# A fused two-layer sequence block on one core: values, next projections, transposes and gates at other half-steps, rounded rows taken from the bank, all second stacks issued by SyncE

## What is computed

```python
def _ada_rmsnorm(x, t, gamma_w, beta_w):
    return (t @ gamma_w.T)[:, None, :] * _rmsnorm(x) + (t @ beta_w.T)[:, None, :]
...
xa = _ada_rmsnorm(x, t, attn_gamma_w, attn_beta_w)
q, k, v = split(xa @ W_q.T), split(xa @ W_k.T), split(xa @ W_v.T)      # 16 heads of 16
attn = softmax(scale * einsum('bnqd,bnkd->bnqk', q, k)); o = einsum('bnqk,bnkd->bnqd', attn, v)
x = x + a_alpha * (o @ W_o.T)
xf = _ada_rmsnorm(x, t, ffn_gamma_w, ffn_beta_w)
x = x + f_alpha * (silu(xf @ gate_w.T) * (xf @ hidden_w.T) @ out_w.T + out_b)
```

## Time and profile before

| | |
|---|---|
| median of 3 runs | 1057.74 us (1053.43 to 1057.96) |
| the profiled execution | 1055.76 us, its span 1054.0 us |
| TensorE busy, granted clock | 996.8 us (95%), 0.968 |
| VectorE, ScalarE, GpSimd busy | 761.7, 536.2, 269.4 us |

### The profile page before, as it was taken

One profiled execution on the slowest core, in us unless ns is written; L12 is line 12 of the kernel. 1 busy time (PEld: TensorE's weight loads), 2 busy tenths in 40 slices (PEclk: granted clock), 3 DMA queues, 4 the chain that ended last, 5 costly groups with the idle time before them and its releaser, 6 DMA issues.

```text
span 1054.0 us, 17114 instructions
## 1 busy us (share of the span) xinstructions
PE 996.8 (95%) x5402; PEld 618.3 (59%) x5402; DVE 761.7 (72%) x1214; ACT 536.2 (51%) x1119; POOL 269.4 (26%) x258
## 2 busy tenths in 40 slices
PE   6999999996999899989989998999899899989988
PEld 4777777773534455645655564556456555645677
DVE  5888788996577777678677767776875877587233
ACT  5466455453555555456445545554564555356421
POOL 1365422221000312132122213221321232122142
PEclk9999999997999899989999998999899899999999
DMA  9544574432420240313022212403130222120000
GB/s 288 144 104 128 141 155 116 120 95 71 111 62 7 59 113 2 81 50 66 11 70 68 47 34 63 98 1 80 51 66 11 72 65 32 62 51 7 11 16 21
DMA packets 93718, 75.11 MB, mean 71 GB/s; under 512 B 44881, under 2 KB 79769, under 8 KB 93665
## 3 DMA queue, kind: packets, MB, share of 16 engines
q1 hardware_dynamic: 79072, 57.20, 20.9%
q10 hardware_dynamic: 14592, 17.25, 7.2%
HBM read 27.73 MB, written 12.61 MB: 38 GB/s over the span
## 4 chain that ended last, share of the span: by engine, by line
PE 78%; DVE 12%; issue 4%; DMA 2%; SPq 1%; ACT 1%; POOL 0%; DVEq 0%; ACTq 0%; POOLq 0%
PE bank L1113 19%; PE bank L362 12%; PE bank L927 10%; PE bank L946 10%; PE bank L1157 8%; PE raw_pair L886 6%; PE bank L812 4%; DVE rowmax L894 3%; PE bank L1007 2%; DVE amax L444 2%; PE bank L385 1%; PE bank L1075 1%; PE bank L862 1%; DVE h L414 1%; DVE x_in L1059 1%
## 5 line engine op out<-in xcount | busy, mean ns | idle before, releaser
L894 DVE TENSOR_REDUCE rowmax<-raw_pair 128x2 f32<-128x1024 f32 x256 | 312.9, 1222 | 127.7 <-PE raw_pair L886 127.7
L935 ACT ACTIVATE probs<-bank 128x512 f32<-128x512 f32 x512 | 281.8, 596 | 230.0 <-PE bank L927 227.7
L886 PE MATMUL raw_pair<-k_stack,q_stack 48*128 48x512 f32 x512 | 177.3, 472 | 24.5 <-DVE rowmax L894 23.7
L927 PE MATMUL bank<-q_stack,k_stack 50*128 50x512 f32 x512 | 197.3, 456 | 2.4 <-DMA q_stack<-shift_rows 1.3
L362 PE MATMUL bank<-up_w,xs_part 128*128 128x512 f32 x768 | 193.3, 405 | 5.7 <-issue 4.5
L362 PEld LDWEIGHTS bank<-up_w,xs_part 128*128 128x128 f32 x768 | 143.4, 192 | 40.5 <-issue 7.4
L946 PE MATMUL bank<-probs,v_ext 128*17 128x512 f32 x1024 | 139.5, 618 | 1.4 <-ACT probs L935 1.2
L1143 POOL TENSOR_TENSOR hid<-scratch,hid 128x512 fp32r<-128x512 f32 x64 | 82.4, 1287 | 217.2 <-ACT hid L1139 217.2
L927 PEld LDWEIGHTS bank<-q_stack,k_stack 50*128 50x128 f32 x512 | 81.7, 190 | 87.4 <-issue 50.3
L1113 PE MATMUL bank<-xf_part,gate_w 128*128 128x512 f32 x384 | 106.0, 411 | 0.8 <-POOL xf_part L1098 0.8
L1113 PE MATMUL bank<-xf_part,hidden_w 128*128 128x512 f32 x384 | 105.3, 409 | 0.0
(11 more groups left out here) (138 smaller groups left out, 1135.1 us busy)
## 6 DMA issues: line engine op xcount, KB each, us to landing
q_stack<-split SPq DMA_DIRECT2D x48, 128.0 KB, 3.0
q_stack<-hid SPq DMA_DIRECT2D x48, 128.0 KB, 2.9
xk<-xT SPq DMA_DIRECT2D x32, 128.0 KB, 3.0
xt<-x_tok SPq DMA_DIRECT2D x32, 128.0 KB, 2.7
x_spill<-x1t ACTq DMA_DIRECT2D x32, 128.0 KB, 2.5
xa_spill<-xa ACTq DMA_DIRECT2D x32, 128.0 KB, 2.3
x_in<-xa_spill SPq DMA_DIRECT2D x8, 512.0 KB, 4.8
k_stack<-split ACTq DMA_DIRECT2D x32, 128.0 KB, 4.8
```

Of the source, the lines that this page charges most:

```text
L886: mm = nc.tensor.matmul(raw_pair[:, half, :], q_stack[rows, slot, qt * P:(qt + 1) * P], k_stack[rows, slot, :], start=True, stop=True)
L894: nc.vector.reduce_max(rowmax[:, e:e + RAWS + 1:RAWS], raw_pair[:], AX.X).then_inc(raw_read, 1)
L927: nc.tensor.matmul(score_bank[c % 3][:], k_stack[rows, slot, kt * P:(kt + 1) * P], q_stack[rows, slot, :], start=True, stop=True).then_inc ...
L935: nc.scalar.activation(probs[:, (kt % 2) * J + j, :], score_bank[c % 3][:], ACT.Exp).then_inc(exp_done, 1)
```

## The change

The table is filled anew: both value modules at half-step 1, q and k of the next batch at 4 and 5, the transposes at 6, the gates and hidden products from 8, and the eight pieces of the last product singly from 24. ScalarE instead of VectorE takes the values out of the banks (`v_act`), and splits the next input at half-step 2; the products of `normed_dve` are shared (two on VectorE, two on ScalarE in `normed_act`) and stand on VectorE ahead of half-step 5's maximum instead of behind it. The feed-forward scale and bias are copied to a tile (`affine_dve`). `xf_act` makes the rounded rows from the bank; `x_in`, which only the difference reads, comes behind it, half on VectorE, half on ScalarE. The first gate waits for the rounded rows, and for the two differences only ahead of the products that use them. SyncE issues all twelve DMAs of the second stacks. `sums_dve` has one more wait, for an operation of the half-steps before.

```diff
-        def split_xa_act(act, c, v_use=None):
+
+        def split_xa_act(act, c):
 
             act.wait_ge(xa_loaded, (c + 1) * 16)
-            if v_use is not None:
-                for m in range(2):
-                    act.wait_ge(pair_free[m], credited(pair_free[m], v_use[m] + 1))
...
-        def stack_sp(sp, m, uses, scores=None):
-
-            for w, rows in ((0, range(ROWS // HD)), (1, range(ROWS // HD - 2))):
+        def stack_sp(sp, m, uses, scores=None, all_rows=False):
+
+            for w in range(2):
                 sp.wait_ge(pair_free[w], credited(pair_free[w], uses[w] + 1))
                 if scores is not None:
                     sp.wait_ge(score_full, scores)
-                for r in rows:
+                for r in range(ROWS // HD - (2 if w == 1 and not all_rows else 0)):
...
-        def v_dve(dve, c, m, use):
-            dve.wait_ge(pv_done, credited(pv_done, c * 16))
-            dve.wait_ge(pair_full[m], use + 1)
-            nc.vector.tensor_scalar(v_ext[:, m * HALF:(m + 1) * HALF, :, 0:HD],
-                                    ab[m][:].rearrange("p (t h d) -> p t h d", t=HALF, d=HD), 1.0, None, ALU.mult) \
+        def v_act(act, c, m, use):
+            act.wait_ge(pv_done, credited(pv_done, c * 16))
+            act.wait_ge(pair_full[m], use + 1)
+            nc.scalar.activation(v_ext[:, m * HALF:(m + 1) * HALF, :, 0:HD],
+                                 ab[m][:].rearrange("p (t h d) -> p t h d", t=HALF, d=HD), ACT.Copy) \
...
         def normed_dve(dve, c, rows=None, normed=None):
             dve.wait_ge(rstd3_done, c + 1)
-            for t in range(T):
+            for t in range(HALF):
                 last = nc.vector.tensor_scalar((normed or normed_rows)(t), (rows or x2)[:, t, :], rstd3[:, t:t + 1], None, ALU.mult)
             last.then_inc(xn3_done, 1)
 
+        def normed_act(act, c, rows=None, normed=None):
+            act.wait_ge(rstd3_done, c + 1)
+            for t in range(HALF, T):
+                last = nc.scalar.activation((normed or normed_rows)(t), (rows or x2)[:, t, :], ACT.Copy,
+                                            scale=rstd3[:, t:t + 1])
+            last.then_inc(xn3_done, 1)
...
         def xf_pe(pe, c, use, normed=None):
-            pe.wait_ge(xn3_done, c + 1)
-            for k in reversed(range(KD)):
+            pe.wait_ge(xn3_done, 2 * c + 2)
+            for k in range(KD):
...
+        def affine_dve(dve, c):
+            nc.vector.tensor_copy(affine[:], par[:, c, FGAM:FGAM + 2 * KD]).then_inc(affine_ready, 1)
+
         def xf_dve(dve, c, use, splits):
 
             dve.wait_ge(q_in_low, credited(q_in_low, splits))
+            dve.wait_ge(affine_ready, c + 1)
+            dve.wait_ge(f_in_high, KD * c + 1)
+            nc.vector.tensor_scalar(x_in[:, :, 0, :], ab[0][:].rearrange("p (t n) -> p t n", t=T),
+                                    affine[:, 0:1], affine[:, KD:KD + 1], ALU.mult, ALU.add).then_inc(pair_free[0], 1)
+
+        def xf_act(act, c, use, splits):
+            act.wait_ge(affine_ready, c + 1)
             for k in range(KD):
-                dve.wait_ge(pair_full[k], use[k] + 1)
-            for k in reversed(range(KD)):
-                nc.vector.tensor_scalar(x_in[:, :, k, :], ab[k][:].rearrange("p (t n) -> p t n", t=T),
-                                        par[:, c, FGAM + k:FGAM + k + 1], par[:, c, FBET + k:FBET + k + 1],
-                                        ALU.mult, ALU.add).then_inc(pair_free[k], 1)
-
-        def xf_act(act, c, use):
-            for k in reversed(range(KD)):
-                act.wait_ge(pair_free[k], credited(pair_free[k], use[k] + 1))
-                nc.scalar.activation(xf_part[0][:, k, :].rearrange("p (t n) -> p t n", t=T), x_in[:, :, k, :],
-                                     ACT.Copy).then_inc(f_in_high, 1)
-
-        def xf_pool(pool, c):
-            for n, k in enumerate(reversed(range(KD))):
-                pool.wait_ge(f_in_high, KD * c + (n + 1))
+                act.wait_ge(pair_full[k], use[k] + 1)
+                nc.scalar.activation(xf_part[0][:, k, :], ab[k][:], ACT.Identity,
+                                     bias=affine[:, KD + k:KD + k + 1], scale=affine[:, k:k + 1]) \
+                    .then_inc(f_in_high, 1)
+            act.wait_ge(q_in_low, credited(q_in_low, splits))
+            nc.scalar.activation(x_in[:, :, 1, :], ab[1][:].rearrange("p (t n) -> p t n", t=T), ACT.Identity,
+                                 bias=affine[:, KD + 1:KD + 2], scale=affine[:, 1:2]).then_inc(pair_free[1], 1)
+
+        def xf_pool(pool, c, use):
+            for k in range(KD):
+                pool.wait_ge(pair_free[k], credited(pair_free[k], use[k] + 1))
...
         def hidden_pe(pe, c, n, f, use, spare=False):
-            pe.wait_ge(f_in_low, credited(f_in_low, KD * (c + 1)))
+            pe.wait_ge(f_in_high, KD * (c + 1))
             pe.wait_ge(pair_free[n], credited(pair_free[n], use + (max(f - 1, 0) if spare else f)))
             weight = (gate_w, hidden_w)[n]
-            for i, (a, wp, k) in enumerate(PROJECTION):
+            for i, (a, wp, k) in enumerate([(a, wp, k) for a, wp in PARTS for k in range(KD)]):
+                if n == 0 and f == 0 and a == 1:
+                    pe.wait_ge(f_in_low, credited(f_in_low, KD * c + (k + 1)))
...
-        V_AT, WO_AT, XF_AT, FFN_AT, OUT_AT = (1, 4), 2, 7, 10, 26
-        Q_AT, K_AT, TO_STACK = 8, 9, 16
-        SPLIT_XA_AT = V_AT[1] + 1
-        OUT_PIECES = ([(0, 0)], [(2, 0)], [(0, 1)], [(1, 0), (1, 1)], [(2, 1)], [(3, 0), (3, 1)])
-
-
-        LAST_PIECES = 4
+        WO_AT, XF_AT, FFN_AT, OUT_AT = 2, 6, 8, 24
+        QK0_AT, TO_STACK = (4, 5), 16
+        OUT_PIECES = ([(0, 0)], [(2, 0)], [(0, 1)], [(1, 0)], [(1, 1)], [(2, 1)], [(3, 0)], [(3, 1)])
+
+
+        LAST_PIECES = 5
...
                 if ffn and h == WO_AT + 3:
+                    affine_dve(dve, b - 1)
                     mean_dve(dve, b - 1)
+                    normed_dve(dve, b - 1)
...
-            stack_sp(sp, 1, both(u, at["qk1"]))
+            stack_sp(sp, 1, both(u, at["qk1"]), all_rows=True)
```

More of the change, by code:

```diff
@@ L1190, in plan @@
             table[0] = [("qk", 1, 0), ("qk", 1, 1)]
-            for m in range(2):
-                table[V_AT[m]] = [("v", m)]
+            table[1] = [("v", 0), ("v", 1)]
             if following:
-                table[Q_AT] = [("qk", 0, 0)]
-                table[K_AT] = [("qk", 0, 1)]
+                for w in range(2):
+                    table[QK0_AT[w]] = [("qk", 0, w)]
             if ffn:
@@ L1302, in act_batch @@
                         squares_act(act, b - 1, m)
-                if following and h == SPLIT_XA_AT:
-                    split_xa_act(act, b + 1, both(u, at["v"]))
-                if ffn and h == XF_AT + 1:
-                    xf_act(act, b - 1, both(u, at["xf"]))
+                if ffn and h == WO_AT + 2:
+                    normed_act(act, b - 1)
+                if ffn and h == XF_AT:
+                    xf_act(act, b - 1, both(u, at["xf"]), b + 2 if following else b + 1)
                 if following and h in (TO_STACK, TO_STACK + 1):
@@ L1338, in dve_batch @@
                     x2_dve(dve, b - 1, 0, u + at["wo"][0])
-                if ffn and h == WO_AT + 3:
-                    normed_dve(dve, b - 1)
+                if ffn and h == XF_AT:
+                    xf_dve(dve, b - 1, both(u, at["xf"]), b + 2 if following else b + 1)
                 for p in done:
@@ L1367, in pool_batch @@
                     normalise_pool(pool, b, 0)
+                if following and h == 2:
+                    split_xa_pool(pool, b + 1)
                 if ffn and h == WO_AT + 3:
                     rstd_pool(pool, b - 1)
-                if following and h == SPLIT_XA_AT:
-                    split_xa_pool(pool, b + 1)
-                if ffn and h == XF_AT + 1:
-                    xf_pool(pool, b - 1)
+                if ffn and h == XF_AT:
+                    xf_pool(pool, b - 1, both(u, at["xf"]))
                     bias_pool(pool, b - 1)
@@ L1456, in act_after @@
                 squares_act(act, B - 1, m, x1_in)
-            xf_act(act, B - 1, (END + 1, END + 1))
+            normed_act(act, B - 1, x1_in, last_normed_rows)
+            xf_act(act, B - 1, (END + 1, END + 1), B)
             for f in range(NH):
```

37 lines of the change are left out of this document (19 added, 18 removed).

## The result

The changed kernel takes **1036.99 us** (median of 4 runs, 1034.72 to 1041.36); the kernel before, beside it on the same chip, 1055.59 (1052.07 to 1057.96). The ratio is 0.983 [0.980, 0.985]. The forecast was 1047.3 with a range of 1036.5 to 1057: the sign was right, the gain of 18.6 us is over twice the 8.5 forecast. The profiled execution took 1034.72 us, the fastest of the four, its span 1032.9; it stands against the 1054.0 of before, 21.1 us less.

A forecast was written before the change was run, and what follows sets the result against it. TensorE's queue was taken to set the time, waiting for `rowmax` that GpSimd's split delays on VectorE. Terms -7.8 - 0.5 + 1.0 - 1.2 = -8.5 from 1055.8 gave 1047.3 us, range 1036.5 to 1057.

The forecast's parts named there:

- The path at full clock: Middle batch without half clock: half-step times summed to 92.6 us, against 95.6 before.
- Behind the last batch: After the last batch, GpSimd no longer holds the first gate and normed rows come 0.4 us sooner: -1.2 us.
- SyncE's queue and the values: Twelve stack DMAs issued by SyncE and value evictions moved to ScalarE: neither was to cost anything.
- the step on the half clock: Middle batches: 3.4 us at half clock, half of it lost, 1.7 us each; bounds none and 3.4 us.
- the term of the middle batches: Six middle batches at 94.3 us each, a gain of 1.3 us (3.0 to -0.4) six times: -7.8 us.
- first rival: The half clock goes away in the middle batches: 6 x 3.0 = 18 us gained, total 1037; chance 0.17.
- The first idle: TensorE waits for `rowmax` before half-step 6's `raw_pair`: 1.6 us instead of 3.7.
- `x2_dve` ... +0.5: Half-step 3: GpSimd's split blocks VectorE's `x2_dve`, which has two SBUF inputs, for 0.5 us.
- The second idle: TensorE waits about 1.2 us while VectorE does half-step 6's `rowmax`, one `x_in` and the next `rowmax`.
- The last batch: No q and k fill half-steps 4 and 5, so TensorE waits longer: +1.0 us (0 to +2).
- The slower one: GpSimd's split, if 2 us later, collides with `x2_dve` and the old half clock stays: 1062; chance 0.11.
- The second rival: The half clock stays as long as it was: total 1053 (1050 to 1056); chance 0.29.

The follow-up runs named there:

- b_split6: The kernel before, with the split of the next attention input at half-step 6 instead of 5: 1039.17 us, ratio 0.986.
- a_stackact: The changed kernel with the last four stack DMAs of the second heads issued by ScalarE again, at half-steps 2 and 3: 1038.32 us.
- a_vdve: The changed kernel with the values taken out of the banks by VectorE again instead of ScalarE: 1039.16 us.
- b_table: The kernel before with only the new table and the wait in `sums_dve`, no operations shared out or rewritten: 1055.36 us, ratio 1.000.
- a_best: a_order with six thrown-away products each at half-steps 4 and 5 of the last batch: 1033.16 us.
- a_late: The changed kernel with two unused reductions, 1.27 us, added on VectorE behind its normed products: 1061.56 us, ratio 1.008.
- a_norm4: The changed kernel with all four normed products on VectorE, none on ScalarE: 1053.52 us, ratio 0.998.
- a_norm4f: a_norm4 with four thrown-away products on TensorE ahead of k's in half-step 5: 1043.56 us, ratio 0.988.
- a_order: a_swap with ScalarE's two normed products moved behind the exponentials of half-step 5: 1035.72 us.
- b_fill: The kernel before with four thrown-away products behind each of half-steps 5 and 6 in batches with feed-forward work: 1053.08 us, ratio 0.998.
- a_swap: The changed kernel with half-step 5's maximum ahead of VectorE's two normed products: 1034.64 us, ratio 0.980.

## Why the forecast was right and wrong

**Right.** *The diagnosis:* GpSimd's split held VectorE's normed products, and through `rowmax` TensorE. b_split6 moves only the split, and 16.2 us go. *The path at full clock:* half-step 5 was to begin 17.05 us after the batch's start and began at 17.11; half-step 6 at 19.3, measured 19.34; half-step 9 at 29.7, measured 29.38; the batch 92.6, measured 92.3. *The price of a stretch at half clock:* 1.7 us, measured about 1.5. *Behind the last batch:* -1.2, measured -1.2, in part by chance: the idle of 0.76 us ahead of the first gate went (0.16 is left inside it), but the idle ahead of the transposes shrank by 0.24 us (2.76 to 2.52), not 0.4. *SyncE's queue and the values:* nothing, and a_stackact and a_vdve show nothing.

**Wrong, and the cause of the miss:** the step on the half clock, "The last batch shows a shorter case, 3.4 us at half clock", and "I take that". The forecast gave each middle batch one stretch, so 94.3 us; the profiled execution had none in any of them, so 92.3. Of the 14.0 us by which the term of the middle batches was short (-7.8 against -21.8), 10.2 are this step (6 x 1.7), 1.8 the path (92.3 instead of 92.6) and 2.0 the reference, below. With the step at none, the prediction's own sum was 1037, its first rival, and the median is 1036.99. So close a hit is chance: the profiled execution took 1034.72, and the misses on the last batch, the first batch and the reference partly cancel. That rival had 0.17 of the chance and the other two clock cases 0.72. The step was weak for two reasons that the runs show. It took the clock as a fixed tax on any thin stretch; the runs show it fall in six, four, two, one or none of six batches, where the idles differ by a few tenths and in part do not differ at all. And it took the length from one stretch of the last batch, where the idles and the work around them are others.

**The reference also was low.** The loop batch that was read lasts 95.6 us; the six together average 95.9 (575.6 / 6). That is 2 us of the 21.8.

**The first idle** was to be 1.6 us and is 1.05. The step "`x2_dve` ... +0.5" measured +0.16, since the split took 2.40 us instead of 2.5 and ended 13.88 us after the batch's start instead of 14.05; the mean came at +17.79 instead of +18.2. The rule on which it rested holds: in b_table the same operation takes 1.19 us against 0.69 two operations behind, with the split from 632.20 on. The Trainium skill, page "SBUF — State Buffer", section "Who interferes with whom", has a VectorE operation with two SBUF inputs contend with a GpSimd one that reads SBUF; these 1.19 us agree.

**The second idle** was to be 1.2 us and is 1.47; both misses together, with the rest, put half-step 9 0.3 us earlier than forecast. That all six batches kept the full clock was luck as much as reserve: in a_stackact, with the same 1.05 and 1.47 us, it fell in four of six.

**The last batch** was to lose 0 to 2 us, 1.0 taken, and lost 3.8. The step counted "1.7 for half clock", one stretch; there are three. Its half-steps 4 and 5 are empty, so TensorE reaches `raw_pair` of half-step 6 early and waits 2.82 us. a_best fills them and gets most of it back. The sign of the danger was seen, its size was outside the bounds. It hid 2.8 us of the other miss.

**The rivals.** The slower one needed a split that ends 2 us later; it ended in time, and no run made it late there. But a_late shows that its price was, if anything, low: 1.2 us of delay on VectorE ends at 1061.6 us, slower than before, where the rival had 2 us give 1062. The second rival, the half clock as long as before (1050 to 1056), is what b_table is: the same table without the sharing, 1055.4.

**What each part of the change is worth.** In the old table the split away from the normed products is enough: b_split6's batch at full clock takes 92.4 us against the change's 92.3, and the whole rest on top of it gives 2.2 us, within the intervals. The new table moves the split away too, and gives nothing alone (b_table). Inside it the shared normed products (16.5) and the rounded rows from the bank (10.9) are large, since they keep the idles short; in the old table they were not tried. Nor was the changed kernel run with its split beside the normed products, or with the first gate's later wait or the single last pieces undone alone.

## What to carry to other kernels

Price a wait of the engine whose clock can fall twice: once as its own length at full clock, and once by whether the granted clock drops behind it, and give the second its own cases (none, as now) ahead of any middle value. When an operation takes three times as long in one place as in another, first see what GpSimd is doing beside it, and try to move that alone; here it was one number. And lay out the idles after a change for all iterations, the last one too: a reordering that feeds the loop can starve the epilogue.

## What the hardware showed that was not expected

- *A small idle costs many times its length, but not at a sharp bound.* 1.05 and 1.47 us of idle (0.86 and 1.66 in the last of them) left the clock at 2.4 GHz in six middle batches of six (the change); the same lengths lost it in four of six with other stack DMAs (a_stackact), and so did 0.88 and 1.47 (a_vdve). 1.58 and 1.61 us lost it in six of six (a_norm4), 0.67 and 1.61 in two of six (a_norm4f): so the longer idle alone does not decide it. In a_order a single 0.85 us lost it in one batch and not in the next. What decides between two batches with like idles stays open; no run was made for it.
- *Filling works in part.* Four thrown-away products per batch, 0.9 us together, brought 10.0 us back in a_norm4f, while eight in b_fill, over a longer idle, brought 2.3. Why the two differ so much was not tried.
- *Less work on the path does not always show.* At full clock a_order's batch is 1.5 us shorter than a_swap's (90.7 against 92.2), nine in all, and its median is no better (1035.7 and 1034.6): the clock fell in four of its six middle batches, in one of a_swap's.
